# Layer 1's value slots in units 2, 4 and 6, and the second store of its keys ahead of unit 7's loads

## The reference

```python
def _L1_xattn_ref(q, k, v, Wq, Wk, Wv, Wo, bo):     # q = layernorm(x), k = v = ctx [2, 2048, 128]
    qh = (q @ Wq.T).reshape(B, QL, 16, 8)
    kh = (k @ Wk.T).reshape(B, KL, 16, 8)
    vh = (v @ Wv.T).reshape(B, KL, 16, 8)
    attn = jnp.einsum('bnhc,bmhc->bhnm', qh, kh) * SCALE
    attn = jax.nn.softmax(attn, axis=-1)
    out = jnp.einsum('bhnm,bmhc->bnhc', attn, vh).reshape(B, QL, DIM)
    return out @ Wo.T + bo
...
x = x + _L0_xattn_ref(_layernorm(x), ctx_1024, mask, ...)
x = x + _L0_attn_ref(_layernorm(x), ...)
x = x + _L0_ffn_ref(_layernorm(x), ...)
x = x + _L1_xattn_ref(_layernorm(x), ctx_1024, ctx_1024, ...)
x = x + _L1_attn_ref(_layernorm(x), ...)
x = x + _L1_ffn_ref(_layernorm(x), ...)
```

## Time and profile before

| | us |
|---|---|
| median of 3 runs | 289.73 |
| lowest and highest | 289.19, 290.54 |
| the profiled execution, its own time | 291.77 |
| its span in the trace | 290.0 |
| TensorE busy | 266.6 |
| VectorE busy | 220.2 |
| ScalarE busy | 207.3 |

### The profile page before, as it was taken

How to read it: one execution, slowest core, us unless ns; L and a number is a source line. 1 busy time by engine, 2 the same in 40 slices (tenths; PEclk the granted TensorE clock), 3 DMA queues, 4 the chain that set the end, 5 groups by cost and what they waited for, 6 DMA issues and landing times.

```text
span 290.0 us, 10305 instructions
## 1 busy us (share of the span) xinstructions
PE 266.6 (92%) x4367; PEld 173.8 (60%) x4371; DVE 220.2 (76%) x375; ACT 207.3 (71%) x427; POOL 81.4 (28%) x155
## 2 busy tenths in 40 slices
PE   6999799999999999977889999899999999868995
PEld 6454467676666675553646776566666655425675
DVE  5887998988888993347799989869899943463582
ACT  7875688999988997544538899869989975431340
POOL 5507661105510383020268161101101030300001
PEclk9999999999999999999999999979999999985999
DMA  7983357632212486330000264413222000000000
GB/s 225 405 335 98 103 162 249 223 101 89 68 60 71 124 292 254 123 97 0 3 2 17 68 222 137 144 55 96 59 77 93 2 5 2 2 1 2 0 0 25
DMA packets 11266, 29.65 MB, mean 102 GB/s; under 512 B 1697, under 2 KB 2817, under 8 KB 10834
## 3 DMA queue, kind: packets, MB, share of 16 engines
q1 hardware_dynamic: 11168, 28.92, 30.0%
q10 hardware_dynamic: 50, 0.03, 0.0%
HBM read 20.42 MB, written 8.52 MB: 100 GB/s over the span
## 4 chain that ended last, share of the span: by engine, by line
PE 68%; DVE 15%; ACT 7%; issue 3%; SPq 2%; DMA 2%; POOL 1%; ACTq 0%; DVEq 0%; POOLq 0%
PE bank L1316 67%; DVE mx L1033 6%; ACT probs L669 2%; DVE s_top L973 2%; DMA k_scratch<-kparts 1%; DMA kpair<-k_scratch 1%; SPq L332 1%; DVE k_rest L990 1%; ACT o_all L591 1%; POOL y L427 1%; DVE s_sb L1224 1%; SPq L360 1%; SPq L334 1%; DVE o_rec L963 1%; DVE xn L935 0%
## 5 line engine op out<-in xcount | busy, mean ns | idle before, releaser
L1033 DVE TENSOR_REDUCE mx<-bank 128x2 f32<-128x1024 f32 x128 | 152.7, 1217 | 17.3 <-PE bank L1316 15.8
L669 ACT ACTIVATE probs<-bank 128x512 f32<-128x512 f32 x256 | 139.6, 596 | 17.8 <-PE bank L1316 13.9
L1316 PE MATMUL bank<-probs,v_all 128*9 128x128 f32 x2048 | 80.7, 275 | 2.3 <-ACT o_all L591 1.5
L1316 PE MATMUL bank<-q_exp,kpair 64*128 64x128 bf16 x1024 | 81.5, 219 | 0.4 <-ACT q_exp L591 0.4
L1316 PE MATMUL bank<-kpair,q_rows 64*128 64x512 bf16 x256 | 71.5, 385 | 4.1 <-DVE mx L1033 1.9
L1316 PEld LDWEIGHTS bank<-q_exp,kpair 64*128 64x128 bf16 x1024 | 55.1, 94 | 26.8 <-ACT probs L669 16.6
L1316 PEld LDWEIGHTS bank<-probs,v_all 128*9 128x9 f32 x2048 | 43.5, 90 | 21.0 <-ACT probs L669 5.6
L528 POOL CAST m_rows<-negm 128x2 bf16<-128x2 f32 x32 | 6.1, 192 | 104.7 <-DVE negm L1040 104.7
L1316 PEld LDWEIGHTS bank<-kpair,q_rows 64*128 64x128 bf16 x256 | 21.9, 94 | 10.6 <-DVE mx L1033 4.2
L427 POOL TENSOR_TENSOR y<-ve,mhalf 128x1 f32<-128x1 f32 (+1 forms) x10 | 5.8, 580 | 40.5 <-DVE ve L922 40.5
L973 DVE TENSOR_REDUCE s_top<-bank 128x8 f32<-128x1024 f32 x8 | 9.4, 1220 | 9.8 <-PE bank L1316 9.8
(11 more groups left out here) (254 smaller groups left out, 325.0 us busy)
## 6 DMA issues: line engine op xcount, KB each, us to landing
kpair<-k_scratch SPq DMA_DIRECT2D x124, 96.0 KB
k_scratch<-kparts SPq DMA_DIRECT2D x16, 256.0 KB, 4.4
k_scratch<-kparts SPq DMA_DIRECT2D x8, 512.0 KB, 4.1
ctxT_s<-in_ctxT SPq DMA_DIRECT2D x4, 512.0 KB, 8.6
mask_s<-in_mask SPq DMA_DIRECT2D x2, 1024.0 KB, 9.5
wM<-in_packM SPq DMA_DIRECT2D x1, 1728.0 KB, 7.6
wB<-in_packB SPq DMA_DIRECT2D x1, 654.0 KB, 4.8
wA<-in_packA SPq DMA_DIRECT2D x1, 256.0 KB, 2.7
```

The costliest lines, as they stand in the source:

```text
L669: act.activation(probs[:, j % 4, :], slot_bank(l, "b", n, j), ACT.Exp).then_inc(S("slot_free"), 1)
L1033: V.tensor_reduce(mx[n % 2][:, w, :], bank[:, 2 * (w % 2):2 * (w % 2) + 2, :], AX.X, ALU.max) \
L1316: return T.matmul(out_, lhsT=lhsT, rhs=rhs, start=start, stop=stop, **kw)
```

## The change

The table `V_UNIT[1]` puts chunks 5, 6 and 7 in units 2, 4 and 6 and no longer in 0, 1 and 2. `V_ROUND` is as it was. In SP's program the store of the second half of batch element 1's keys moves from behind unit 7's loads to between unit 6's and unit 7's, which is how layer 0 has it.

```diff
-V_UNIT = ({3: 6, 5: 7}, {0: 5, 1: 6, 2: 7})
+V_UNIT = ({3: 6, 5: 7}, {2: 5, 4: 6, 6: 7})
...
             for n in range(6):
                 cross_k(1, n)
-            store_k(1, 1, 0)
-            cross_k(1, 6)
-            cross_k(1, 7)
-            store_k(1, 1, 1)
+            for half in range(2):
+                store_k(1, 1, half)
+                cross_k(1, 6 + half)
             for n in range(8, NN):
                 cross_k(1, n)
```

## The result

| | before | after |
|---|---|---|
| median, us | 291.64 | 288.37 |
| lowest to highest | 288.07 to 295.24 | 287.04 to 290.21 |
| executions | 20 | 20 |
| profiled execution, its own time | 291.77 | 287.10 |
| its span | 290.0 | 285.3 |

The ratio is 0.9935, 95% interval 0.9907 to 0.9963: 0.65% faster, 1.9 us of 290. The ratio leaves out executions of either kernel more than 1.5% above its fastest, and these are mostly executions of before; the medians, over all 20, are 3.3 us apart, and the means 3.0 (interval 2.1 to 3.9). The forecast was 2.3 us less, 287.4; the median is 288.37. The three runs known ahead had a median of 289.73, while the 20, these three among them, have 291.64, so the base of the sum was low.

What follows compares the result with a forecast made beforehand. TensorE, busy 92% of the span, was taken to set the pace nearly everywhere. Store -3.28, slots out -1.2, slots in +2.16 gave -2.3 us: 287.4 from a median of 289.73, range 286.1 to 289.6.

Steps and rivals of the forecast that it cites:

- The stall at unit 8: Layer 1's cross-attention: TensorE's 1.84 us delay at unit 8's first score pair goes once the store moves earlier.
- The moved wait and its margin: SP's wait for the last key split, now ahead of the store, is already met, with 1.4 us to spare.
- rival C: The moved store delays unit 7's loads: 0.8 us new stall, perhaps a 1.44 us clock drop; middle 288.9; chance 0.11.
- Slots out of units 0 and 1: Removing two value slots there saves 1.2 us of their 2.16, 0.3 of it by unit 1's put_exp.
- Slots into units 4 and 6: TensorE has no gap there, so each added value slot costs its full 1.08 us, 2.16 together.
- The clock: The granted clock drop behind unit 8's stall, 188.55 to 193.97, costs 1.44 us more and goes with the stall.
- Rival B: The clock drop behind unit 8's stall is absent in the timed runs: only 0.9 us less, 288.8; chance 0.22.
- The base: Forecast started from the timed median 289.73, taking the profiled execution's 291.77 as 2.0 us above it.
- Rival D: New TensorE idle time in layer 1's units 0 and 1 drops the clock: 2.9 us slower, 292.6; chance 0.07.

Runs made afterwards that it cites:

- after_again: The full change measured once more against the kernel before, in the rounds of the single-half kernels: median 288.69 us, ratio 0.9958.
- after_tail: The full change plus eight idle products in layer 1's self-attention: median 287.63 us.
- fill_quiet: Kernel before plus eight idle products in layer 1's self-attention and repeated score matmuls in layer 0 unit 0's waits and layer 1 unit 8's: median 288.17 us.

## Why the prediction was right or wrong, point by point

**The stall at unit 8: right.** 1.84 us was read from the trace; the wait for keys is gone in every trace with the moved store, and with the store as the only difference the executions at 0.999 or above differ by 1.3 us (286.0 beside 287.3), 2.3 and 1.6 us in the medians of three comparisons.

**The moved wait and its margin: right.** 1.4 us were expected between the split and the store; it is 1.6.

**Unit 7's loads (rival C): right not to expect it.** The store's issue takes 2.29 us, and with the loads right behind it TensorE doesn't wait for unit 7's keys. The Trainium skill, "DMA: Bandwidth & Descriptors", section "Queues, rings and completion order", has descriptors of a queue consumed in ring order on each DMA engine. No run here shows or contradicts that order: the store took 5.6 us right behind four loads and 4.1 us when they had been issued 3 us earlier, but nearly all of the difference lay in its issue. What the trace shows is that behind the store there was room enough.

**Slots out of units 0 and 1: right, 1.1 us for the predicted 1.2,** by the two steps named, 0.3 at unit 1's put_exp with 0.72 us of wait, and the rest up to the pair of unit 4, which starts at 164.95, 0.19 us behind the scores ahead of it, because VectorE's reduction before it ends only at 164.81.

**Slots into units 4 and 6: right, 1.09 us each.**

**The clock: the mechanism was right, the term was mis-sized.** The step "1.44 us more" behind the stall was carried into the sum whole, from one execution. Filling the wait alone shows that it is worth 1.0 us on average, 0.1 to 1.8: the drop comes in about half of the executions. With the terms as measured the sum is -1.84 - 1.0 - 1.1 + 2.2 = -1.7 us. Measured were 1.9 by the ratio, which sees little of the clock, and by the means 3.0 in the first comparison (2.1 to 3.9) and 1.9 in after_again (0.7 to 3.2). So the sum may be short by a part of the first comparison's 3.0; the runs don't say whether that part is chance. Rival B was the other half of this truth and not a case of its own: it is not that timed runs are free of the drop, but that each execution has it or not. The Trainium skill's page "TensorE: Matmul & The Clock Gate", Part 1, which says that the monitor runs freely, fits: the same program gave clocks of 0.965 to 1.000.

**The base: wrong, and this is the step that failed.** "It stands 2.0 above the median of the timed runs" took the profiled execution for a slow one and the median of three for the typical. It was the reverse: 20 executions have a median of 291.64, and the 110 of the later comparisons, on four chips, one of 291.1, so 291.77 was ordinary and 289.73 was low. The step also took the clock drop off whole from a base that, being 2.0 us below an execution with the drop, could hardly have it in every execution. From the kernel's true median, 287.4 would have been 4.2 us or 1.5% less, where 1.9 us (0.65%) by the ratio and 3.3 us (1.1%) by the medians were measured. That the number itself is only 1.0 us too low is in part luck: the base was 1.9 us low, and the medians lie 0.9 us further apart than the forecast's 2.3. With three executions of a kernel whose times spread over 7 us, the range ought to have had the base's own doubt in it.

**Rival D: not what happened, but the evidence against it was too thin.** Waits of under 1 us in a first unit can cost the clock: behind layer 0's waits of 0.83 and 0.50 us it fell in the profile of after_again and not in the one that the prediction quoted. Whether layer 1's unit 0, with its waits of 0.43, 0.37, 0.36 and 0.72 us, ever pays for it in the changed kernel wasn't isolated; in the profile of after it did not, and after_tail had 4 of 12 executions below full clock. This stays open.

**The profiled execution** came out 4.7 us below before, of which the sum explains 2.3. The rest is mostly self-attention in layer 1, at half clock before and at full clock after, with the same 2.16 us wait in both. Nothing in the change bears on it, so it is put down to chance; that is argued, not shown.

## What to carry to other kernels

A transfer that gates a later unit belongs in the queue at the point where its data are ready, ahead of loads whose buffers come free later. Work that hides nothing is cheapest where TensorE waits anyway: moving the value slots from units with waits to units without cost 1.1 us net, and the store alone was the better change. Before forecasting a per cent, look at how far single executions of the same kernel lie apart and why; here filling TensorE's waits with idle products was worth as much as the change itself (fill_quiet, which only fills waits, is 0.56% below before by the ratio and 3.0 us by the medians, the change 0.65% and 3.3).

## What the runs showed of the hardware

Behind one wait of 1.2 to 1.5 us of TensorE, in work otherwise almost without a gap, the granted clock fell in about half of the executions, and over 290 us the kernel before was at full clock in 8 executions of 110. Executions of one kernel on one chip lay up to 9 us apart (287.42 to 296.70), the granted clock going from 1.000 to 0.965 with them; but at a clock of 0.999 or above the 11 of fill_quiet still spread over 2.4 us. The same 1 MB store took 4.1 us from first issue to landing when the loads ahead of it had been issued 3 us earlier, and 5.6 us right behind four loads of 96 KB, 1.4 of the 1.5 us between them in its issue by SP.
